# Half 0's layer norm in two batches, the second batch's rows normed by ScalarE

## The reference

```
xn = _layernorm(x, axis=-1)                      # (x - mean) / sqrt(var + 1e-5)
s  = recurrence over time of xn                  # long convolution with a decaying phasor
logits = xn @ router_w                           # 32 experts
topk_w, topk_idx = top_k(softmax(logits), 4)
routed = sum over the 4 experts of  topk_w * (silu(xn @ w_gate) * (xn @ w_up)) @ w_down
sh = (silu(xn @ sh_gate) * (xn @ sh_up)) @ sh_down * sigmoid(xn @ sh_gate_w)
x  = x + s * silu(routed + sh)
# second layer: norm, attention, a mixture of 8 experts with 2 chosen, x = x + s * silu(...)
```

## Time and profile before

| | |
|---|---|
| median of 3 executions | 444.82 us (443.53 to 445.05) |
| the profiled execution | 442.83 us, of which span 441.1 |
| TensorE, DVE, ScalarE, GpSimd busy | 381.2, 310.5, 256.3, 301.3 us |
| mean granted clock of TensorE | 0.933 |

### The profile page before, as it was taken

The page is one execution under the profiler, slowest core; times in us unless marked ns, Lnnn a source line. Parts: engine busy times, 40 slices in busy tenths (PEclk is TensorE's granted clock), DMA queues, the critical chain, the costliest instruction groups (busy, mean ns, idle before and its releaser), DMA issues. The chain is left out here.

```text
span 441.1 us, 8741 instructions
## 1 busy us (share of the span) xinstructions
PE 381.2 (86%) x2604; PEld 345.9 (78%) x2604; DVE 310.5 (70%) x1113; ACT 256.3 (58%) x504; POOL 301.3 (68%) x364
## 2 busy tenths in 40 slices
PE   2928976994799999987999998988997998889994
PEld 1716975893399999986999998977986987779984
DVE  7986789779066766672757585774589989896633
ACT  2503214430056767662766664667797986889882
POOL 7977777777777777764777777727777877208710
PEclk9975997797799999995999998998999999999998
DMA  8989996111467766546577664422111112002200
GB/s 261 388 220 291 259 407 247 54 50 52 151 184 219 212 225 208 180 142 207 167 226 209 201 190 149 130 100 55 52 52 48 50 48 55 25 1 72 73 25 25
DMA packets 45902, 65.17 MB, mean 148 GB/s; under 512 B 8585, under 2 KB 23330, under 8 KB 45858
## 3 DMA queue, kind: packets, MB, share of 16 engines
q1 hardware_dynamic: 30322, 35.24, 26.3%
q0 software_dynamic: 8192, 16.79, 12.9%
q10 hardware_dynamic: 7344, 12.59, 7.9%
HBM read 28.93 MB, written 35.65 MB: 146 GB/s over the span
## 5 line engine op out<-in xcount | busy, mean ns | idle before, releaser
L556 POOL DMA_INDIRECT slot_rows<-xn_tok,slot_of x128 | 126.9, 991 | 41.2 <-issue 38.6
L570 POOL DMA_INDIRECT onehot<-expert_rows,slot_of x64 | 65.1, 1018 | 33.2 <-issue 18.9
L570 POOL DMA_INDIRECT route_tmp<-expert_rows,slot_of x64 | 63.8, 997 | 19.5 <-issue 19.5
L1464 DVE TENSOR_TENSOR act<-sg,ps 128x384 f32<-128x384 f32 x48 | 26.6, 553 | 50.7 <-ACT sg L1051 50.4
L763 PE MATMUL ps<-w_dn,actT 96*128 x384 | 52.2, 280 | 1.3 <-ACT zeros L1060 1.3
L763 PEld LDWEIGHTS ps<-w_dn,actT 96*128 96x128 f32 x384 | 47.5, 195 | 1.7 <-issue 1.7
L1051 ACT ACTIVATE sg<-ps 128x384 f32<-128x384 f32 x48 | 23.5, 490 | 37.0 <-PE ps L772 36.9
L772 PE MATMUL ps<-w_gu,raw_fc 128*128 x192 | 38.2, 345 | 0.7 <-DVE act L1464 0.5
L1060 ACT COPY zeros<-ps 128x512 f32<-128x512 f32 x48 | 28.1, 586 | 15.6 <-PE ps L763 15.4
L772 PE MATMUL ps<-w_gu,raw_pr 128*128 x192 | 35.8, 330 | 0.2
L772 PEld LDWEIGHTS ps<-w_gu,raw_fc 128*128 128x128 f32 x192 | 33.0, 202 | 1.6 <-issue 1.6
(11 more groups left out here) (244 smaller groups left out, 921.5 us busy)
## 6 DMA issues: line engine op xcount, KB each, us to landing
slot_rows<-zeros SPq DMA_DIRECT2D x12, 1024.0 KB, 12.5
rows<-slot_rows SPq DMA_DIRECT2D x48, 256.0 KB, 2.9
expert_rows<-zeros ACTq DMA_DIRECT2D x48, 256.0 KB, 2.2
x_tok<-in_L_attn_x_dram SPq DMA_DIRECT2D x8, 256.0 KB, 5.9
slot_rows<-xn_tok,slot_of POOLq DMA_INDIRECT x128
out_dram<-w_gu SPq DMA_DIRECT2D x16, 128.0 KB, 1.8
w_dn<-in_L_ffn_w_down_dram SPq DMA_DIRECT2D x1, 1536.0 KB, 17.3
onehot<-expert_rows,slot_of POOLq DMA_INDIRECT x64, 2.7
```

Source lines behind the costliest of these rows:

```text
L556: g.indirect_dma_start(out=slot_rows[r], out_offset=bass.IndirectOffsetOnAxis(ap=slot_of[:, n:n + 1], axis=0), in_=xn_tok[:, r * HT + t, : ...
L570: g.indirect_dma_start(out=gath[b % 4][:, j, :], out_offset=None, in_=expert_rows[r], in_offset=bass.IndirectOffsetOnAxis(ap=slot_of[:, n: ...
L1464: v.tensor_tensor(act[u][:].rearrange("p (a b) i -> p a b i", a=2), sg[u][:].rearrange("p (a b) i -> p a b i", a=2), ps[:, 1 + 2 * u:3 + 2 ...
```

## The change

Half 0's statistics and root are made for eight rows, then for the other eight. The second eight's `bn_stats` run beside the first root, the first eight's norm rows beside the second root. The second eight rows are normed by ScalarE as x * rstd + shift, with shift = -mean * rstd from DVE. TensorE turns groups 0 and 1, makes their logits, then turns and makes logits for groups 2 and 3 one after the other, each after `rest_normed`. Half 1 goes as before, though the functions are cut otherwise. GpSimd clears `gate_parts` after all scatters instead of before.

```diff
-            g.memset(gate_parts[:], 0.0).then_inc(parts_zero, 1)
...
                             in_=xn_tok[:, r * HT + t, :], in_offset=None).then_inc(sent[r], 16)
+            g.memset(gate_parts[:], 0.0).then_inc(parts_zero, 1)
...
+            def turn_group(it):
+                if it >= 2:
+                    pe.wait_ge(xT_sb, it - 1)
+                for j in range(GT):
+                    mm = pe.transpose(ps[:, it % 2, j * P:(j + 1) * P], xn_tok[:, it * GT + j, :], ident[:])
+                mm.then_inc(xT_ps, 1)
+
+            def turn_first():
+                for it in range(2):
+                    pe.wait_ge(xn_ready, it + 1)
+                    turn_group(it)
+                for it in range(2):
+                    logits_of(it)
+                for it in range(2, NG // NH):
+                    pe.wait_ge(rest_normed, it - 1)
+                    turn_group(it)
+                    logits_of(it)
...
             pe.wait_ge(stats_done, 1)
             warm(3)
-            turn_half(0)
+            turn_first()
             ranks(0)
...
+            def norm_group(it):
+                if it == 2:
+                    sc.wait_ge(rest_ready, 1)
+                for t in range(it * GT, (it + 1) * GT):
+                    last = a.activation(xn_tok[:, t, :], x_tok[:, t, :], ACT.Identity,
+                                        bias=shift[:, t - HT // 2:t - HT // 2 + 1], scale=rstd[:, t:t + 1])
+                last.then_inc(rest_normed, 1)
+
+            def copy_first():
+                copy_turned(0)
+                copy_turned(1)
+                copy_logits(0)
+                norm_group(2)
+                copy_logits(1)
+                norm_group(3)
+                for it in (2, 3):
+                    copy_turned(it)
+                    copy_logits(it)
...
-            copy_half(0)
+            copy_first()
+            gate_shared(0)
             exp_top(0)
...
+            def finish_stats(T0, T1, lk):
...
+            def norm_first():
+                H = HT // 2
+                for t in range(H):
+                    last = row_stats(t)
+                    if t == H - 3:
+                        last.then_inc(stats_done, 1)
+                link(last)
+                marks = []
+                finish_stats(0, H, chain.link_beside(lambda n: marks.append(chain.mark(row_stats(H + n))), H))
+                chain.after(marks[-1])
+
+                def first_row(n):
+                    last = norm_row(n)
+                    if n % GT == GT - 1:
+                        last.then_inc(xn_ready, 1)
+                finish_stats(H, HT, chain.link_beside(first_row, H))
+                v.scalar_tensor_tensor(out=shift[:], in0=mean[:, H:HT], scalar=-1.0, in1=rstd[:, H:HT],
+                                       op0=ALU.mult, op1=ALU.mult).then_inc(rest_ready, 1)
...
-            norm0(0)
+            norm_first()
             dve.wait_ge(pool_c, 7)
             route(0)
```

More of the change, by code:

```diff
@@ L199, in build @@
         rtmp = sb("rtmp", [P, 2 * NT])
+        shift = sb("shift", [P, HT // 2])
         top8 = sb("top8", [P, HT, 8])
@@ L312, in build @@
         stats_done = sem("stats_done")
+        rest_ready = sem("rest_ready")
+        rest_normed = sem("rest_normed")
         nearly_sent = sem("nearly_sent")
@@ L625, in tile_ids, with turn_second @@
                 pe.transpose(ps[0:1, 7, 0:ST], tile_ex[0:ST, :], ident[0:ST, 0:ST]).then_inc(exT_row, 1)
-            def turn_half(r):
-                for it in range(r * NG // NH, (r + 1) * NG // NH):
-                    pe.wait_ge(xn_ready, it + 1)
[L630 to L634, removed]
+            def turn_group(it):
[6 more added lines that the diff above has]
+                for it in range(2):
+                    pe.wait_ge(xn_ready, it + 1)
+                    turn_group(it)
[5 more added lines that the diff above has]
+                    logits_of(it)
+            def turn_second():
+                for it in range(NG // NH, NG):
+                    pe.wait_ge(xn_ready, it - 1)
+                    turn_group(it)
                     if it % (NG // NH):
                         logits_of(it - 1)
-                logits_of((r + 1) * NG // NH - 1)
+                logits_of(NG - 1)
             pe.wait_ge(stats_done, 1)
             warm(3)
-            turn_half(0)
+            turn_first()
             ranks(0)
@@ L706, in _ @@
                 shared_out(it, it % 2)
-            turn_half(1)
+            turn_second()
             for b in range(EARLY):
@@ L999, in exp_top, with copy_turned, copy_second, gate_shared @@
                 a.activation(tw[:], tw[:], ACT.Exp).then_inc(tw_exp, 1)
[L1001 to L1004, removed]
+            def copy_turned(it):
+                sc.wait_ge(xT_ps, it + 1)
+                a.copy(xnT[:, it * GW:(it + 1) * GW], bank(it % 2)).then_inc(xT_sb, 1)
+            def norm_group(it):
[15 more added lines that the diff above has]
+                    copy_logits(it)
+            def copy_second():
+                for it in range(NG // NH, NG):
+                    copy_turned(it)
                     if it % (NG // NH):
                         copy_logits(it - 1)
-                copy_logits((r + 1) * NG // NH - 1)
+                copy_logits(NG - 1)
+            def gate_shared(r):
                 sc.wait_ge(lg_sb, (r + 1) * NG // NH)
@@ L1033, in _ @@
                 if it == NSEQ // NH:
-                    copy_half(1)
+                    copy_second()
+                    gate_shared(1)
                     for b in range(EARLY):
@@ L1249, in row_stats, with norm_row, norm0 @@
                 return v.bn_stats(stats[:, t, :], x_tok[:, t, :])
-            def norm0(r, beside=None):
-                beside = beside or (lambda k: None)
+            def finish_stats(T0, T1, lk):
+                m, va, t = mean[:, T0:T1], var[:, T0:T1], rtmp[:, 0:T1 - T0]
+                s = stats[:, T0:T1, :]
+                lk(v.tensor_tensor(t, s[:, :, 1], s[:, :, 4], ALU.subtract))
+                v.tensor_tensor(va, s[:, :, 2], s[:, :, 5], ALU.add)
+                v.tensor_tensor(m, s[:, :, 1], s[:, :, 4], ALU.add)
+                lk(v.tensor_tensor(t, t, t, ALU.mult))
+                v.tensor_scalar(m, m, 0.5, None, ALU.mult)
+                lk(v.tensor_scalar(t, t, 0.25, EPS, ALU.mult, ALU.add))
+                lk(v.scalar_tensor_tensor(out=va, in0=va, scalar=1.0 / P, in1=t, op0=ALU.mult, op1=ALU.add))
+                rsqrt_steps(nc, lk, rstd[:, T0:T1], va, rtmp[:, 0:2 * (T1 - T0)])
+            def norm_row(t):
+                return v.tensor_scalar(xn_tok[:, t, :], x_tok[:, t, :], mean[:, t:t + 1], rstd[:, t:t + 1],
+                                       ALU.subtract, ALU.mult)
+            def norm_first():
[15 more added lines that the diff above has]
+                                       op0=ALU.mult, op1=ALU.mult).then_inc(rest_ready, 1)
+            def norm0(r, beside):
                 T0, T1 = r * HT, (r + 1) * HT
@@ L1258, in norm0 @@
                         beside((t - T0) // 4)
-                    if t == HT - 2:
-                        last.then_inc(stats_done, 1)
                 link(last)
[L1262 to L1272, removed]
+                finish_stats(T0, T1, link)
                 for t in range(T0, T1):
-                    last = v.tensor_scalar(xn_tok[:, t, :], x_tok[:, t, :], mean[:, t:t + 1], rstd[:, t:t + 1],
-                                           ALU.subtract, ALU.mult)
+                    last = norm_row(t)
                     if t % GT == GT - 1:
```

## The result

The changed kernel takes 451.62 us (450.17 to 452.66) where the kernel before takes 444.20 (the median of four executions; 444.82 was that of the three of them known ahead): a ratio of 1.0165, 95% interval 1.0132 to 1.0197. Its profiled execution took 451.97 us, with a span of 450.2. Forecast were 451.9 and a range of 446.6 to 455.0.

What follows compares the result with a forecast made beforehand. The start of half 0's scatters, set by its slot numbers, was taken to bound the kernel; TensorE's later ranks and slower clock shift it 7.1 us, so 444.82 + 7.1 = 451.9 us, range 446.6 to 455.0.

Steps and rivals of the forecast that it cites:

- Where the time is set: Half 0's slot numbers start GpSimd's scatters; any shift of the first scatter moves the end one for one.
- Rival B: TensorE's clock falls in half 0's longer turn: shift +5 to +10 us, 7.1 taken, median 451.9; chance 0.68.
- rival A: TensorE's clock stays up, only the longer order costs: +2.5 to +3.3 us, median 447.3 to 448.1; chance 0.2.
- Rival C: Not slower: DVE's order counts and it is free 0.6 us earlier, at best 444.2 us; chance 0.12.
- TensorE's first rank group: Half 0's ranks on TensorE: starting later than 19.5 us they set the end; 22.05 forecast with the clock up.
- ScalarE's norm row: ScalarE's eight norm rows in half 0: 0.26 us each taken, 0.37 as the upper end.
- The clock's fall: TensorE's granted clock in half 0's turn and logits: fall to 0.50 expected between 16 and 20 us.
- The clock's return: TensorE's clock comes back 5 us after gapless matmuls start, here at 29.3 us, during half 0's ranks.
- First top-8: DVE's first pick group in half 0 starts at 16.15 us, 0.15 earlier than before.
- The second root: DVE's root for the second eight rows, beside eight norm rows: 11.0 to 15.7 us, 3.6 + 1.1.
- The clear: GpSimd's 0.95 us clear, moved behind the last scatter into idle time: nothing gained, nothing lost.
- up to 3.9 is absorbed: DVE's 3.92 us idle before its first shared-expert product takes up the shift; beyond that half 1's routing slips.

Runs made afterwards that it cites:

- e3: Kernel before with five extra-long waits' worth of clears of gate_parts on GpSimd between the first slot numbers and first scatter; 448.63 us beside 443.64, ratio 1.0115.
- e5: Changed kernel without the filler matmul between half 0's rank groups; ratio 1.0060 to the kernel before.
- e4: Changed kernel with four more filler matmuls in TensorE's gaps around the turns of groups 0, 2 and 3; ratio 1.0039 to the kernel before.
- a2: The changed kernel measured once more, nothing altered; ratio 1.0164 to the kernel before.
- e7: Changed kernel's two batches and early fillers, but DVE norms all rows and TensorE keeps the old order; 449.97 us beside 443.64, ratio 1.0132.
- e6: Changed kernel with rank groups 0 and 1 between turns and logits of groups 2 and 3, and fillers in gaps; 444.32 us beside 443.64, ratio 1.0003.
- e8: As e6, but DVE norms the third group, ScalarE only the fourth, and a filler follows group 2's turn; 443.89 us beside 443.34, ratio 1.0000.
- e2: Kernel before without its three filler-matmul calls' warm(3) ahead of half 0's turn; 448.77 us beside 445.08, ratio 1.0096.

## Why the prediction was right

**Where the time is set** held. The change acts through the start of the scatters, and goes from there to the end (e3: 5.42 us in, 5.0 out; only in e5 does the time lie clearly below its scatters' shift).

**Rival B, the likeliest, is what happened**, and e4 separates its two parts. The order, with ScalarE's norm rows, has 2.62 us of the first scatter, where rival A had 2.5 to 3.3; the clock adds 4.05. Predicted were 7.1 in all, measured 6.67 at the scatter (8.19 in a2) and 7.4 in the median.

**Rival C fell at the place the prediction named.** DVE came free at 15.2, half a microsecond earlier even than forecast (15.8), and had no use of it. TensorE's first rank group, whose limit was 19.5, stood at 22.55 with the clock up.

**Three terms were mis-sized, and two of them cancelled.**

- ScalarE's norm row: 0.26 us taken and 0.37 as the upper end, 0.39 measured. The upper end was that of one column operand alone, and two columns cost more than that. The Trainium skill, "ScalarE: Activation LUTs", section "What ACT_TABLE_LOAD costs", gives 0.39 us here and 479 ns for one alone, both estimates worked out from its figures; the trace has 0.39 and 481. There the page was the better source, and the nearest row was the wrong kind of neighbour. Eight rows at 0.13 us more are 1.0 us ahead of the third group's copy; logits 2 started at 19.79 where 19.0 was forecast, though ScalarE had begun 0.2 us early. In e4, with the clock up, DVE's third pick group waited 1.21 us where I had 0.3.
- The clock's fall: expected between 16 and 20, measured 14.6, 13.6, 14.0 and 14.0 (after, a2, e5, e7). The reason given, that the new stretch is longer and sparser up to 22 us, is not what decided: e7, with the old order of turns and logits, fell at the same place, and the kernels with a filler behind the first turn (e4, e6, e8) did not fall there. So the first logits, too, ran at 0.50, in 3.14 us for 16 instead of 1.92. With the norm rows this set the ranks to 25.02 where 24.3 was forecast.
- The clock's return: 28.3 instead of 29.3, so ranks and fillers took 6.96 us to the scan and not 7.75. This gave back what the two others had cost, and the scan came at 31.98 where 32.05 was forecast. In a2, where the return came at 30.6, it didn't, and the scan stood at 33.50, still within the bound of +10.

So the close agreement of the median is partly luck; the range, +1.8 to +10, is what the working was worth.

**The rest.** First top-8 at 16.12 (16.15 forecast), two errors again: the first logits started at 14.28, half a microsecond ahead of the forecast, and the early fall of the clock took that back (in e4, with the clock up, it is 15.75; in a2, where the fall came earlier, 16.87). The second root with eight rows beside it took 4.43 us from 10.64 to 15.07 (4.7 forecast); about half of the difference lies in the steps that have a row beside them and half in the seven bare steps behind them, 1.42 us where seven of before take 1.56. The clear cost nothing, as expected. At DVE's first shared-expert product the 3.92 us of idle were used up whole (it starts at 46.52 with no wait), 2.68 us later than before. That "up to 3.9 is absorbed" did not hold beyond this point: half 1's last logits started at 75.76 instead of 69.51, 6.25 us later and so nearly the whole shift. It could not be seen in half 1's first experts, which wait for the scattered rows and moved about as the scatters did.

## What to carry to other kernels

Work that is given to another engine to free one must be followed to the first thing that everyone waits for: here DVE gained half a microsecond at a place where only logits could use it, while the rows given away went into one series (norm, turn, copy, logits, ranks) on two other engines. Matmuls that only keep TensorE's clock up are part of the schedule: whoever moves what starts them, moves the clock's fall as well, and the price (at the first scatter 4.1 us of 6.7 here, 5.4 in e2) can be larger than all that was meant to be saved. Where the gap lies counts too: one filler behind the first turn kept the clock up after a pause of 1.54 us ahead of it. And a queue that is written out in order, like the ranks behind the last logits with a filler between each two, must be written again when the times of its inputs change; e6 got all but 0.84 us of the scatters' shift back by order and fillers alone, and e8 the rest with four norm rows given back to DVE.

## What the runs showed of the hardware

- An activation with both scale and bias from a column takes 481 ns for 128 x 128 f32, 0.39 us from one to the next; with one column 367 ns and 0.26.
- Between the fillers and the fall to 0.50 (after, a2, e5, e7) TensorE had four transposes with 0.8 to 1.3 us of idle ahead of them and 0.7 to 0.8 behind, and then the next transposes and logits. In the kernel before, transposes and logits follow the fillers without a pause, and nothing fell. Nor did it in e4, e6 and e8, with 1.0 to 1.5 us of idle ahead of the four transposes and a filler of 1.0 us behind them. So a filler in the second gap, of 0.7 us, was enough at this place, and 4 to 5 us hang on it; whether the clock would have held without the later fillers of these runs, none shows.
- Part of the difference in the moment of the fall goes with the fillers' own time: six of them took 4.65, 4.85, 4.90 and 5.18 us in a2, e7, e5 and after, and the fall came at 13.6, 14.0, 14.0 and 14.6. What makes the fillers differ between executions no run here shows.
- Back-to-back f32 transposes and logits from 14.6 to 22.9 did not bring the clock back in e7. It rose at 27.7 there, at 28.3 in after, 30.6 in a2 and 31.1 in e5, with ranks from 22.95, 25.02, 25.77 and 25.60: 3.3 to 5.5 us into them. The 5 us that I had taken from one place of half 1 were of the right size, but no constant.
- The granted clock of a stretch must be read beside durations. In e2 the record says 1.00 from the start, while eight logits take 1.8 us, as they do at 0.50 elsewhere, and the first eight transposes 2.06 us instead of 1.36. So that e2's logits ran at half speed is read from their durations. The kernel before has the same at its first fillers: 0.89 us each, 0.46 later, with 1.00 on record from 8 to 13 us. The stretch of e2, with the granted clock as the third number from the end:

```profile
16.00:20.00 4.00, 4.00 (x21) 4.00 (x22) 2.56 (x18) 1.12 (x3) 3.64 (x13) 1.00 1.05 399
```
